# Two-block transformer kernel: expert low parts and bias products to VectorE and TensorE, nine merges to GpSimd

## What is computed

```python
x = x + tanh(g_xattn) * xattn(layernorm(x), ctx)          # 16 heads of 16, causal
x = x + tanh(g_ffn) * ffn(layernorm(x))                   # x: (4, 256, 256) float32

def ffn(h0):                                              # D = 256, H = 16, HD = 128
    h = h0 + attention(layernorm(h0))                     # causal, rope, out @ wo + bo
    x = layernorm(h).reshape(-1, 256)                     # 1024 tokens
    raw = softmax(x @ w_gate)                             # 4 experts
    vals, idx = top_k(raw, 2); w = softmax(vals)
    comb = zeros.at[token, idx].add(w)
    hmid = gelu(einsum('td,edi->tei', x, we1) + be1)      # I = 256
    eout = einsum('tei,eid->ted', hmid, we2) + be2
    return h + einsum('te,ted->td', comb, eout)
```

## Time and profile before

| what | us |
|---|---|
| median of 3 runs | 465.79 |
| the runs | 462.73 to 468.49 |
| the profiled execution's own time | 467.53 |
| its span, first to last instruction | 465.70 |
| mean granted TensorE clock, share of full | 0.983 |

### The profile page before, as it was taken

One profiled execution on the slowest core, in us unless ns is written; L12 is line 12 of the kernel. 1 busy time (PEld: TensorE's weight loads), 2 busy tenths in 40 slices (PEclk: granted clock), 3 DMA queues, 4 the chain that ended last, 5 costly groups with the idle time before them and its releaser, 6 DMA issues.

```text
span 465.7 us, 10305 instructions
## 1 busy us (share of the span) xinstructions
PE 415.1 (89%) x3135; PEld 361.4 (78%) x3150; DVE 364.4 (78%) x1124; ACT 286.3 (61%) x655; POOL 301.2 (65%) x433
## 2 busy tenths in 40 slices
PE   0477997998899899999999999999999996598994
PEld 0366876886776799899899898998998986586994
DVE  3854568677789797897798788888888877928997
ACT  3357674755235777587677677677677675375440
POOL 5898959720598487587587687677677555343551
PEclk9999999999999899999999999999999998989998
DMA  5600000200256875775865865855955655000011
GB/s 153 189 3 2 1 3 2 92 2 1 46 113 125 174 149 119 174 150 108 203 143 106 189 136 118 196 131 108 225 119 109 145 80 112 4 0 2 1 45 45
DMA packets 71795, 44.53 MB, mean 96 GB/s; under 512 B 57424, under 2 KB 60112, under 8 KB 71760
## 3 DMA queue, kind: packets, MB, share of 16 engines
q1 hardware_dynamic: 67680, 35.42, 36.1%
q10 hardware_dynamic: 4080, 8.69, 6.5%
HBM read 13.68 MB, written 1.05 MB: 32 GB/s over the span
## 4 chain that ended last, share of the span: by engine, by line
PE 68%; DVE 17%; issue 5%; ACT 4%; POOL 3%; DMA 2%; ACTq 0%; SPq 0%; DVEq 0%; POOLq 0%
PE bank L1464 36%; PE bank L1532 5%; PE bank L1582 5%; DVE yacc L1309 3%; PE bank L1531 3%; PE bank L1583 3%; DVE yacc L1318 2%; PE bank L1404 2%; PE bank L1445 2%; POOL room L523 2%; PE bank L1359 2%; PE bank L1380 2%; PE bank L1405 1%; DMA qk_room<-qk_room 1%; PE bank L1426 1%
## 5 line engine op out<-in xcount | busy, mean ns | idle before, releaser
L799 ACT ACTIVATE probs<-sm,nm 128x128 f32<-128x128 f32 (+1 forms) x128 | 57.0, 447 | 44.1 <-DVE nm L1184 43.8
L789 ACT ACTIVATE probs<-turned 128x768 uint16<-128x768 uint16 x60 | 64.7, 1078 | 18.1 <-DMA turned<-halves 16.5
L1464 PE MATMUL bank<-hH,qk_parts 128*128 128x512 f32 x240 | 75.4, 395 | 0.0
L536 POOL COPY halves<-probs 128x768 uint16<-128x768 uint16 x64 | 52.6, 822 | 33.0 <-DVE probs L1208 31.1
L523 POOL TENSOR_TENSOR room<-room,qk_room 128x512 f32<-128x512 f32 x32 | 41.2, 1290 | 35.6 <-DMA qk_room<-qk_room 30.6
L1464 PE MATMUL bank<-hL,qk_parts 128*128 128x512 f32 x120 | 57.7, 481 | 0.9 <-DVE room L1105 0.9
L1464 PEld LDWEIGHTS bank<-hH,qk_parts 128*128 128x128 f32 x240 | 45.2, 188 | 9.5
L1105 DVE SCALAR_TENSOR_TENSOR room<-bank,qk_bias,cst_sb 128x512 f32<-128x512 f32 x64 | 47.5, 742 | 0.0
L1076 DVE TENSOR_REDUCE nxm<-bank 128x2 bf16<-128x512 f32 (+1 forms) x48 | 32.8, 688 | 18.1 <-PE bank L1405 17.5
L523 POOL TENSOR_TENSOR room<-room,q_room 128x512 f32<-128x512 f32 x32 | 41.1, 1287 | 5.5 <-DMA q_room<-q_room 5.5
L684 ACT ACTIVATE probs<-bank 128x512 f32<-128x512 f32 x48 | 28.3, 595 | 25.4 <-PE bank L1421 14.4
(11 more groups left out here) (241 smaller groups left out, 1291.8 us busy)
## 6 DMA issues: line engine op xcount, KB each, us to landing
qk_room<-qk_room SPq DMA_DIRECT2D x64, 128.0 KB, 2.4
q_room<-q_room SPq DMA_DIRECT2D x64, 128.0 KB, 2.4
stg<-in_wqkv ACTq DMA_DIRECT2D x6, 768.0 KB, 5.8
stge<-in_we ACTq DMA_DIRECT2D x7, 256.0 KB, 3.1
stg<-in_wqkv SPq DMA_DIRECT2D x2, 768.0 KB, 5.2
stgo<-in_wo ACTq DMA_DIRECT2D x6, 256.0 KB, 3.4
x_sb<-in_x SPq DMA_DIRECT2D x4, 256.0 KB, 4.1
turned<-halves SPq DMA_TRANSPOSE x64, 2.8
```

The source lines that it names most:

```text
L536: pool.tensor_copy(halves[:, j % 2, :, :], PR[:, j % 2, 0:384].bitcast(U16).rearrange("p (n h) -> p h n", h=2)).then_inc(s["b_split"], 1)
L789: act.activation(*merged(j - 3), ACT.Copy).then_inc(s["b_merge"], 1)
L799: ins = act.activation(PR[:, q, a:e], sm[:, q, a:e], ACT.Exp, bias=nm[:, q, t:t + 1], scale=-1.0, accum_out=rs[:, q, t:t + 1])
L1464: ins = pe.matmul(outp, l, r, start=(m == 0), stop=(m == n - 1))
```

## The change

- **Merges.** `LATE` goes from NU - 4 to NU - 9: the merges of units 55 to 63 run on GpSimd; those of 55 to 59 were on ScalarE. On GpSimd, step T now does merge(T-3) ahead of split(T). `PTs` has four slots instead of two, so a late merge waits for the values of unit u-4 instead of u-2.
- **Maxima.** From unit 59 on, `maxima(T+1)` stands in VectorE's step T, ahead of normalise(T). The last o_high, o_low, output_add and second_norm change places.
- **Low parts.** All `hidden_low2` and `middle_low` move from GpSimd's program to VectorE's; GpSimd has nothing to do once the experts run.
- **Gates.** tanh(g_ffn) is folded into the gates, and 1 / (1 + exp(d)) becomes 0.5 g (1 + tanh(-d/2)). The residual y x tanh(g) + x (`residual_form`) is taken before the experts are added, two of four times inside the gate chain. Tanh stands behind the next gelu, not behind the first Exp.
- **Bias products.** The 32 operations with be2 rows (line 1309) become products on TensorE: gates are packed (high, low, high), turned (`pack_turn`), copied by VectorE, and eight matmuls (`second_bias`) with 12 contracted rows give gates x be2 in banks 4 and 5; VectorE adds the banks (`add_biases`, two operations of 128x512 a chunk). be2 is loaded early (12 small DMAs on SP behind the first attention's last q parts), and cut into parts by five GpSimd operations in steps 16 to 20 (`bias_rows`) and two small VectorE reductions.

The diff, cut to its core:

```diff
-        LATE = NU - 4
+        LATE = NU - 9
@@ SP
+            sp.wait_ge(s["q_parts"], 2 * B)
+            for q in range(4):
+                for r in range(3):
+                    row = 32 * q + E * r
+                    sp.dma_start(be2_raw[row:row + E, :], be2).then_inc(s["d_be"], 16)
-            sp.dma_start(be2_rows, be2.rearrange("(o e) n -> o e n", o=1).to_broadcast([P, E, D])).then_inc(s["d_be"], 16)
@@ GpSimd
             def merge(u):
-                pool.wait_ge(s["b_pv"], u - 1)
+                pool.wait_ge(s["b_pv"], u - 3)
+                if U * i + j - 3 >= LATE:
+                    merge(U * i + j - 3)
                 if unit(i, j, 0):
                     split(i, j)
+                if i == 2 and j < 5:
+                    bias_rows(j)
+            merge(NU - 5)
             split(NP - 1, 6)
             merge(NU - 4)
...
-            hidden_low2(0)
-            hidden_low2(1)
-            for n in range(2 * NE):
-                if n in (2, 3):
-                    hidden_low2(n)
-                middle_low(n)
@@ ScalarE
-                if unit(i, j, 3):
+                if unit(i, j, 3) and not (isinstance(i, int) and U * i + j - 3 >= LATE):
                     merge(i, j)
...
-                    act.activation(gate[:, 400:408], gate[:, 392:400], ACT.Exp).then_inc(s["c_gexp"], 1)
+                    act.activation(gate[:, 400:408], gate[:, 392:400], ACT.Tanh, scale=-0.5).then_inc(s["c_gexp"], 1)
@@ VectorE
+            AHEAD = NU - LEAD
-                if unit(i, j, 0) and not (isinstance(i, int) and T == 0):
+                if unit(i, j, 0) and not (isinstance(i, int) and (T == 0 or T > AHEAD)):
                     maxima(i, j)
+                if isinstance(i, int) and T >= AHEAD:
+                    maxima(*divmod(T + 1, U))
...
+            hidden_low2(0)
+            second_norm(2, 0)
+            hidden_low2(1)
+            second_norm(3, 0)
+            for phase in range(1, 6):
                 second_norm(2, phase, 2)
+            middle_low(0)
+            middle_low(1)
...
+            middle_low(5)
+            accumulate(0)
+            middle_low(6)
+            accumulate(1)
+            middle_low(7)
+            hidden_low2(2)
+            hidden_low2(3)
+            dve.wait_ge(s["c_pack_pe"], 1)
+            dve.tensor_copy(gates_turned, bank[4][:, 0:256]).then_inc(s["c_gT"], 1)
+            residual_form(2)
+            residual_form(3)
+            add_biases(0)
+            accumulate(2)
+            for m in range(3, 2 * E):
+                middle_low(2 * m + 2) if m < 2 * E - 1 else None
+                middle_low(2 * m + 3) if m < 2 * E - 1 else None
+                accumulate(m)
+                if m == 5:
+                    add_biases(1)
@@ TensorE
-            expert_out(0)
+            expert_out(0, (0,))
             pe.wait_ge(s["c_lgT"], 1)
...
+            expert_out(0, (1,))
             expert_out(1)
             middle(4)
             middle(5)
             middle(6)
-            for n in range(7, 2 * NE):
+            middle(7)
+            pack_turn()
+            expert_out(2)
+            for n in range(8, 2 * NE):
                 middle(n)
+                if n == 8:
+                    second_bias(0)
+                if n == 12:
+                    second_bias(1)
                 if n % 2:
                     expert_out((n - 3) // 2)
```

More of the change, by code:

```diff
@@ L1252, in _, with hidden_low2, middle_low @@
             output_add(LAST + 3, 3)
-            for phase in range(6):
+            def hidden_low2(b):
+                dve.wait_ge(s["c_hH"], b + 1)
+                cut = slice(256 * b, 256 * (b + 1))
+                dve.tensor_tensor(hL[:, :, cut], h2T[:, :, cut], hH[:, :, cut].bitcast(F32), ALU.subtract).then_inc(s["c_h"], 1)
+            def middle_low(n):
+                dve.wait_ge(s["c_gH"], n + 1)
+                dve.tensor_tensor(GL[:, (n // 2) % 2, n % 2, :], G[:, n % 2, :], GH[:, (n // 2) % 2, n % 2, :].bitcast(F32),
+                                  ALU.subtract).then_inc(s["c_gL"], 1)
+            hidden_low2(0)
[3 more added lines that the diff above has]
+            for phase in range(1, 6):
                 second_norm(2, phase, 2)
+            middle_low(0)
+            middle_low(1)
             Gt = lambda a, n: gate[:, a:a + n]
@@ L1296, in _, with accumulate @@
             link(dve.tensor_tensor(Gt(0, 32), Gt(120, 32), Gt(152, 32), ALU.add))
-            dve.wait_ge(s["d_be"], 16)
-            dve.wait_ge(s["b_yadd"], NU // 2)
-            for m in range(2 * E):
+            packed = nh[:, 1, :].rearrange("p (t b w) -> p b t w", t=2, w=32)
+            gates = gate[:, 0:32].rearrange("p (b t e) -> p b t e", b=B, e=E)
+            link(dve.tensor_copy(packed[:, :, :, 0:E].bitcast(F32R), gates))
+            dve.tensor_copy(packed[:, :, :, 2 * E:3 * E], packed[:, :, :, 0:E])
+            dve.tensor_tensor(packed[:, :, :, E:2 * E].bitcast(F32R), gates, packed[:, :, :, 0:E], ALU.subtract).then_inc(s["c_pack"], 1)
+            def accumulate(m):
                 c, e = divmod(m, E)
@@ L1320, in _, with add_biases @@
                     ins.then_inc(s["c_acc"], 1)
-                    if e == E - 1:
-                        dve.wait_ge(s["c_acc"], 2 * m + hf + 1)
-                        y = yacc[:, 2 * b:2 * b + 2, :].rearrange("p t n -> p (t n)")
-                        xb = x_sb[:, 2 * b:2 * b + 2, :].rearrange("p t n -> p (t n)")
-                        dve.scalar_tensor_tensor(y, y, small[:, 97:98], xb, ALU.mult, ALU.add).then_inc(s["c_fin"], 1)
+            def add_biases(c):
+                dve.wait_ge(s["c_be"], c + 1)
+                for hf in range(2):
+                    b = 2 * c + hf
+                    dve.wait_ge(s["c_acc"], 2 * (E * c + 1) + hf + 1)
+                    y = yacc[:, 2 * b:2 * b + 2, :].rearrange("p t n -> p (t n)")
+                    dve.tensor_tensor(y, y, bank[4 + hf][:, :], ALU.add).then_inc(s["c_badd"], 1)
+            middle_low(5)
[17 more added lines that the diff above has]
+                    add_biases(1)
         @block.tensor
@@ L1630, in middle, with expert_out @@
                 middle_part(n, 0, 512).then_inc(s["c_mid"], 1)
-            def expert_out(m):
+            def expert_out(m, parts=(0, 1)):
                 c, e = divmod(m, E)
@@ L1636, in expert_out @@
                     pe.wait_ge(s["b_yadd"], NU // 2)
-                for hf in range(2):
+                for hf in parts:
                     if m >= 2:
@@ L1644, in expert_out, with pack_turn, second_bias @@
                     ins.then_inc(s["c_exp_pe"], 1)
+            def pack_turn():
+                pe.wait_ge(s["c_pack"], 1)
+                for t in range(2):
+                    ins = pe.transpose(bank[4][:, t * P:(t + 1) * P], nh[:, 1, t * P:(t + 1) * P], ident)
+                ins.then_inc(s["c_pack_pe"], 1)
+            def second_bias(c):
+                if c == 0:
+                    pe.wait_ge(s["c_gT"], 1)
+                    pe.wait_ge(s["be2_step"], 5)
+                else:
+                    pe.wait_ge(s["c_badd"], 2)
+                for hf in range(2):
+                    rows_ = slice(32 * (2 * c + hf), 32 * (2 * c + hf) + 3 * E)
+                    for t in range(2):
+                        ins = pe.matmul(bank[4 + hf][:, 256 * t:256 * (t + 1)], gates_turned[rows_, t * P:(t + 1) * P], be2_parts[rows_, :],
+                                        start=True, stop=True)
+                ins.then_inc(s["c_be"], 1)
             pe.wait_ge(s["we_ready"], NP // 2)
```

99 lines of the change are left out of this document (60 added, 39 removed).

## The result

| | before | after | ratio [95%] |
|---|---|---|---|
| median of 20 executions each | 466.78 (462.73 to 468.63) | 463.65 (462.12 to 465.62) | 0.9948 [0.993, 0.9967] |
| profiled execution | 467.53, span 465.7, clock 0.983 | 462.98, span 461.2, clock 0.996 | |

The kernel became 0.5% faster, 2.4 us by the ratio. The forecast was 461.5, 0.9%: right sign, inside the wide range of 456.3 to 466.5 but above the forecast's own 459.5 to 463, and nearly twice the measured gain. The profiled execution, however, came out at 462.98 where the working had 463.2 for it. The walk's total met the profiled execution to a few tenths, in good part by luck, and the number for the median was missed; the experiments are about how both can be true.

The account below looks back on a forecast made before the run. Attention's end was bound by a chain across engines, the experts by VectorE and TensorE together. -3.6 and -0.7 made -4.3 us: profiled 467.53 to 463.2, less 1.7 for the median, 461.5; range 456.3 to 466.5.

Parts of the forecast that it names:

- Stage A, -3.6: End of the attention, up to the first expert matmul at 405.89: 3.0 to 4.1 us shorter, middle taken.
- Merges, +1.55: End of attention: merge(55) queues on GpSimd behind the last rope addition, so unit 55's values start 1.55 us later.
- Blocking, +2.0: Last attention steps: VectorE's normalise products wait for GpSimd copies, four partial meetings of 0.2 to 0.8 us, +2.0.
- Minima ahead, -3.9: Last attention steps: exponentials run while VectorE normalises, so its 3.9 us of waiting for ScalarE go.
- The last units: End of attention: last merge ends at 394.65, last wo product starts 2.4 to 3.5 us earlier, at 397.0 to 398.1.
- Stage B, -0.7: Experts, 405.89 to the span's end at 465.70: TensorE's work, waits of 2.9 us and the end total 59.1, against 59.8.
- Early edits, 0: Before the last 90 us: be2's small loads, five GpSimd operations and two VectorE reductions cost 0, GpSimd's at most 3.2 us.
- Tables, 0: ScalarE in the experts: Tanh behind a gelu needs no table load, taken as 0, with +2.0 the other end.
- that rival: Experts' gates on ScalarE: Tanh needs its own table loads, +2.0 us, giving 463.5; chance 0.18.
- Blocking: Rival, last attention steps: normalise products wait for whole GpSimd merges, 7.35 us instead of 2.0, giving 466.9; chance 0.13.
- The clock stays up: Rival, start of the experts: TensorE holds its upper clock level, -2.5 us, giving 459.0; chance 0.21.
- The change does little: Rival: waits at the attention's end only change names and the experts give 0.7, giving 465.1; chance 0.11.

Follow-up runs that it names:

- filled kernel before: Kernel before the change plus useless matmuls (16, 10, 18) in TensorE's waits at about 388, 399 and 403 us: median 464.67, ratio 0.9951 to before.
- filled against filled: Changed kernel with useless matmuls (6, 10, 14) in its three waits, median 463.44, set against the filled kernel before, 464.67.

## Why the prediction came out as it did

**The sum is the step that failed**: "The profiled execution took 467.53 ... it would take 463.2. The median of the runs, 465.79, lies 1.7 under it: 461.5." That carries a gain read from one execution over to the median by a parallel shift. It holds only if the profiled execution and the median one lose the same things, in both kernels. They did not. The median of before, over twenty executions and not three, is 466.78, so its profiled execution lay 0.75 us above it; the profiled one of the changed kernel lay 0.67 under its own. The 4.55 us from profile to profile are thus 3.13 from median to median. All executions of before that were measured beside the experiments (97), by granted clock over the span:

| mean granted clock | executions | median us |
|---|---|---|
| up to 0.984 | 14 | 468.00 |
| 0.985 to 0.988 | 31 | 467.36 |
| 0.989 to 0.992 | 32 | 465.17 |
| 0.993 and more | 20 | 463.38, 463.05 from 0.996 on (two) |

Time and clock have a correlation of -0.86. The profiled execution, at 0.983, belonged to the slowest class, 14 of 97. The filled kernel before shows what it had lost: 1.4 us in stage A and 1.3 in stage B, together 2.7 (of which the forecast named 1.0, for the product at 390.61, and took the rest as work). That the executions around the median had lost only part of that, so that the change could give back only part, is read from this table and not shown by a trace of them. After the change the twenty executions had clocks of 0.993 (11, median 464.54), 0.996 (7, 463.20) and 1.0 (2, 462.40): the profiled one, at 0.996, stands under their median too.

By the filled kernels the clock is 1.8 us (466.45 to 464.67) and the edits are about 1.2; measured were 2.4 by the ratio and 3.1 by the medians. So most of what was measured is that the clock falls less often. The stages agree with the 1.2: -1.7 and -0.2, filled against filled, and +0.9 for be2's parts make -1.0. At equal mean clock, though, even the sign of the edits' own share is open: at 0.993 fourteen executions of before took 463.4 and eleven of the changed kernel 464.5, while only kernels with the change reach 1.0. What the edits are worth by themselves is not settled.

That the walk met the profiled time was luck in good part. Of its 4.3 us it had 1.0 for the clock and 3.3 for the edits; the profiles had 2.7 for the clock in the last two stages, and the edits gave about 1. It also took nothing for the stages before, and was met there because two things cancelled: the profile of before had a fall of the clock near 156 us that the other did not have (units 8 to 16 took 33.33 and 32.53 us), and be2's parts cost the changed kernel as much (units 16 to 24: 33.56 and 34.31).

That the clock falls in a wait ahead of matmuls, and that the matmuls behind it start at the lower level, the Trainium skill tells too, of waits for a DMA (TensorE: Matmul & The Clock Gate, section "HAM oscillation — how this bites in real kernels"). The trace agrees for waits on other engines: the first expert matmuls of before stand 0.21 us apart behind the 2.77 us wait at 405.89, and 0.12 apart in the filled kernel before.

**Stage A, -3.6.** Profile to profile it was -2.9, the profiled clock's 1.4 among it; filled against filled -1.7.
- *Merges, +1.55*: right in place and size (1.57). But with four merges this cost and most of the blocking go (3.4 us of it become 0.8), and stage A is only 0.5 us shorter, since 3.5 us of waiting for exponentials come back; the terms of the sum are not independent.
- *Blocking, +2.0*: about right. In the last six units the normalise products of 128x128 took up to 0.94 us (0.29 alone) and those of 128x256 up to 1.16 (0.35 alone), each beside a GpSimd copy; together they lose 3.4 us, 1.6 more than in the kernel before. The Trainium skill also has it that a VectorE operation by a scalar can take both ports of SBUF, one of which it shares with GpSimd, and that the later of the two then waits for the whole of the other (SBUF — State Buffer, section "Who interferes with whom"). The trace agrees: 0.34 us at 387.41 alone, and 1.13 at 388.64 beside the copy of 388.58.
- *Minima ahead, -3.9*: the largest mis-sized term, 1.7 to 2.2, with 1.2 us of clock in it. The wait was counted away whole, and what VectorE and TensorE wait for next (2.1 for scores, 3.5 for merges) was priced only by merge(55).
- *The last units*: near the forecast, the last merge 0.1 us early and the last wo product 0.1 us past its upper bound.

**Stage B, -0.7.** Profile to profile -1.5; filled against filled -0.2. Three waits were mis-sized, +0.5 together, as much as the difference between -0.7 and -0.2. The wait for the second norm was 1.04, not 0.3; that for the first bank 0.71, not 0.4; that for hidden_low2(3) 1.69, not 2.2. VectorE's costliest groups of the changed kernel from 400 us on:

```profile
L1367 DVE SCALAR_TENSOR_TENSOR yacc<-bank,gate,yacc 128x256 f32<-128x256 f32 x32 | 13.5, 477 | 1.1 <-PE bank L1537 1.1
L1279 DVE TENSOR_TENSOR qk_parts<-G,o_parts 128x512 fp32r<-128x512 f32 x16 | 10.8, 687 | 8.4 <-ACT o_parts L913 8.3
```

The subtraction is 0.69 us, from a bound of 0.67 to 1.26: right. VectorE gave up 20.4 us and stage B got almost nothing for it, since TensorE was full too: that step was right.

**Early edits, 0**: wrong by about +0.9 us, for be2's parts. "GpSimd has 2.6 us of 10 free" was an average; behind them TensorE waits for GpSimd's low part of wv.

**Tables, 0**: right. ScalarE in the changed kernel, start, us, instruction:

```profile
416.46 1.28 ACT L908 ACT_TABLE_LOAD   x1
421.08 0.69 ACT L908 ACTIVATE G<-bank,cols_sb 128x512 f32<-128x512 f32 x1 [3.33 <-PE bank L1537]
421.80 0.63 ACT L913 ACTIVATE o_parts<-G 128x512 fp32r<-128x512 f32 x1
422.33 0.19 ACT L903 ACTIVATE gate<-gate 128x8 f32<-128x8 f32 x1
422.48 0.69 ACT L908 ACTIVATE G<-bank,cols_sb 128x512 f32<-128x512 f32 x1
```

The Tanh at 422.33 stands between two gelus with no load, and the whole trace has four as before. The page of the Trainium skill that was weighed there (ScalarE: Activation LUTs, "Table sets: the hidden batching unit") lists tanh elsewhere; the measurement decides, and that rival is out. Its 463.5 is the number nearest to the measured 463.65, by luck.

**The other rivals.** *Blocking* did not grow beyond its term. *The clock stays up* was half true in the wrong place. It held through stage A (1.00 in 390 to 400) and fell from 404 on; but filled, without that fall, the stage from first expert matmul to the gate product takes as long (9.56 against 9.58). The fall costs nothing there, since TensorE is ahead of VectorE's second norm (in the kernel before it cost 0.6 us over the same stretch). With four late merges the expert matmuls ran at full clock and then waited longer, in its timeline of TensorE:

```profile
407.49 0.88 PE L1683 MATMUL bank<-cst_sb,nh 128*128 128x128 f32 x4 [2.30 <-DVE nh L1175]
```

Its price of -2.5 was therefore none. *The change does little* (465.1, a gain of 0.7) came as near to the measured 2.4 as the forecast's 4.3 did: waits of stage A did change names, but stage A still gained. The range was set a little short of its own rivals, since blocking stood at 466.9 and the range ended at 466.5; it made no difference.

What stays open: what the edits are worth at equal clock; why before with only its first two waits filled was late early on; and why executions of one kernel at one clock still lie about 2 us apart (before at 0.986: 465.6 to 469.3), under which gains of less than 1 us are lost.

## What to carry to other kernels

Before a gain read from one profiled execution is put onto a median, place that execution among the runs by its granted clock; what it lost to the clock is not there to be gained in the others. Where TensorE's clock falls behind short waits in some executions, a few matmuls into an unused bank are a cheap trial (here as much as the whole change), and they help to compare two kernels. A wait that is removed is worth what its engine and its readers wait for next, not its length: here 3.9 us of waiting gave 2, more than half of it through the clock, and the kernel with four merges kept 3.5 us of the same waits and was no slower.

## What the runs showed of the hardware

- Filling three waits with 44 matmuls that nobody reads moved the median by 1.8 us; filling only the first two left the fall at the experts, filling only the third moved it, and neither gave a gain.
- A fall of the clock near 156 us, in a stretch that no experiment but the last edits, came in 7 of the 13 profiles without the filler there, of nearly the same program. Two kernels, before and then after, columns as in the earlier trace rows:

```profile
152.00:160.00 8.00, 5.98 (x26) 5.05 (x26) 6.95 (x25) 6.91 (x16) 4.93 (x6) 0.79 0.71 144
```

```profile
152.00:160.00 8.00, 5.74 (x32) 4.67 (x31) 6.93 (x27) 6.71 (x16) 5.27 (x8) 1.00 0.73 145
```

  With it units 8 to 16 took 33.3 to 34.4 us, without it 32.5 to 32.9 (33.2 with the filler there). So nearly the same program loses about 1 us there or not, by the execution; the filler there took the fall away and gave only part of that back.
- Tanh needs no table load behind a gelu here; a load of 1.28 us is followed by its first activation 0.02 us later.
- A matmul with only 12 contracted rows is no quicker than a full one: four of 256 columns start at 432.49 and the next matmul at 432.92, 0.11 us each, where full ones of 256 columns stand 0.12 apart.
